# When GpSimd's adds wait for VectorE's low parts, and later work comes in halves: a two-layer graph kernel on one core

## The reference

```python
def _gcn_layer(x, adj, W, b):
    d_inv_sqrt = (jnp.sum(adj, axis=1) + 1e-09) ** (-0.5)
    msg = d_inv_sqrt[:, None] * adj * d_inv_sqrt[None, :] @ x
    return jax.nn.relu(msg @ W + b)
H_f = _gcn_layer(feature_x, adj, W_f, b_f)      # feature_x is x
H_s = _gcn_layer(spatial_x, adj, W_s, b_s)
attn = jax.nn.sigmoid(jnp.concatenate([H_f, H_s], axis=1) @ W_att + b_att)
x = _layernorm(x + attn * H_f + (1.0 - attn) * H_s)
# x, spatial_x: 4096 x 128, W_f, W_s: 128 x 128, all float32
```

## Time and profile before

| | us |
|---|---|
| median of 3 runs | 392.65 (392.62 to 392.72) |
| profiled execution | 393.04 |
| its span | 391.2 |
| PE busy in the span | 378.3 (97%) |
| DVE / ACT / POOL busy | 303.2 / 285.6 / 155.3 |

### The profile page before, as it was taken

One profiled execution on the slowest core, in us unless ns is written; L12 is line 12 of the kernel. 1 busy time (PEld: TensorE's weight loads), 2 busy tenths in 40 slices (PEclk: granted clock), 3 DMA queues, 4 the chain that ended last, 5 costly groups with the idle time before them and its releaser, 6 DMA issues. The chain is left out here.

```text
span 391.2 us, 5501 instructions
## 1 busy us (share of the span) xinstructions
PE 378.3 (97%) x1778; PEld 314.0 (80%) x1778; DVE 303.2 (77%) x443; ACT 285.6 (73%) x381; POOL 155.3 (40%) x204
## 2 busy tenths in 40 slices
PE   7889999999999999999999999999999999999992
PEld 7667778788888888788888888888788888888992
DVE  2789997999578975769578583928976796889795
ACT  3668788888877887878878887778742666687556
POOL 2332611571066402670058220010100417877795
PEclk9999999999999999999999999999999999999997
DMA  8999999999999999999999999999775534445002
GB/s 268 423 417 424 420 412 421 423 419 418 421 416 421 423 418 420 421 420 422 418 423 420 424 414 423 413 390 415 232 281 208 213 108 160 164 157 168 4 25 81
DMA packets 24556, 130.77 MB, mean 334 GB/s; under 512 B 2640, under 2 KB 7632, under 8 KB 10448
## 3 DMA queue, kind: packets, MB, share of 16 engines
q1 hardware_dynamic: 24528, 130.43, 83.2%
HBM read 128.32 MB, written 2.10 MB: 333 GB/s over the span
## 5 line engine op out<-in xcount | busy, mean ns | idle before, releaser
L533 DVE TENSOR_TENSOR Al<-raw,Ah 128x2048 fp32r<-128x2048 f32 (+2 forms) x101 | 162.0, 1620 | 40.3 <-ACT Ah L721 40.2
L408 PE MATMUL sums<-Ah,Yh 128*128 128x512 f32 (+1 forms) x484 | 186.9, 386 | 1.3 <-DVE Al L533 1.3
L409 PE MATMUL sums<-Ah,Yl 128*128 128x512 f32 (+1 forms) x484 | 185.1, 382 | 0.0
L410 PE MATMUL sums<-Al,Yh 128*128 128x512 f32 (+1 forms) x484 | 185.0, 382 | 0.0
L721 ACT ACTIVATE Ah<-raw 128x2048 fp32r<-128x2048 f32 (+2 forms) x101 | 127.1, 1283 | 48.9 <-DMA raw<-in_At 29.9
L731 ACT ACTIVATE nat<-nat 128x2048 f32<-128x2048 f32 (+1 forms) x54 | 100.1, 1855 | 20.0 <-DMA nat<-in_adj 19.3
L408 PEld LDWEIGHTS sums<-Ah,Yh 128*128 128x128 f32 x484 | 91.0, 188 | 22.5 <-DVE Al L533 4.8
L410 PEld LDWEIGHTS sums<-Al,Yh 128*128 128x128 f32 x484 | 91.0, 188 | 17.9
L409 PEld LDWEIGHTS sums<-Ah,Yl 128*128 128x128 f32 x484 | 91.0, 188 | 17.1
L553 DVE TENSOR_TENSOR acc<-sums,acc 128x512 f32<-128x512 f32 (+1 forms) x122 | 76.8, 673 | 28.8 <-PE sums L410 25.2
L871 POOL TENSOR_TENSOR S<-S,raw 128x512 f32<-128x512 f32 x40 | 62.4, 1559 | 32.2 <-DMA raw<-in_At 29.2
(11 more groups left out here) (56 smaller groups left out, 201.2 us busy)
## 6 DMA issues: line engine op xcount, KB each, us to landing
raw<-in_At SPq DMA_DIRECT2D x63, 1024.0 KB, 9.8
nat<-in_adj SPq DMA_DIRECT2D x47, 1024.0 KB, 12.0
nat<-in_adj SPq DMA_DIRECT2D x8, 768.0 KB, 9.6
xs<-in_xs SPq DMA_DIRECT2D x5, 512.0 KB, 11.1
out<-xs SPq DMA_DIRECT2D x15, 128.0 KB, 1.8
xs<-in_xs SPq DMA_DIRECT2D x5, 256.0 KB, 11.5
nat<-in_adj SPq DMA_DIRECT2D x2, 512.0 KB, 6.6
raw<-in_At SPq DMA_DIRECT2D x2, 512.0 KB, 8.5
```

The source lines that it names most:

```text
L408: pe.matmul(to, Yh[:, t % YRING, hs], high, start=first, stop=False)
L409: pe.matmul(to, Yl[:, t % YRING, hs], high, start=False, stop=False)
L410: mm = pe.matmul(to, Yh[:, t % YRING, hs], low, start=False, stop=last)
L533: dve.tensor_tensor(Al[:, k % SPLITS, a * IB:b * IB], raw[:, k % RAWS, a * IB:b * IB], Ah[:, k % SPLITS, a * IB:b * IB], ALU.subtract).the ...
```

## The change

Five things change:

1. In items under 14 that have adds, POOL waits before the first add: for Yl of the item's new tile where it has one (items 2, 6, 11, 13), otherwise for all low parts of the items before it (items 1, 5, 10, 12).
2. In items under 14 with a new tile, Ah and Al are made in four pieces of 512 instead of 512, 512, 1024.
3. Items 22 to 49 are made in two pieces of 1024 instead of one of 2048, and PE takes their first block in `first_block`. `HALVED` is split in two names for this: `BY_BLOCK` (22) for the order of sweeps and evacuations, `IN_PARTS` (50) for the pieces.
4. x of groups 3 to 7 is loaded three items later: after items 22, 29, 37, 46, 48 instead of 19, 26, 34, 43, 45.
5. Around item 48 DVE's order changes: one run (`LATE`, run 55) is evacuated last, the low parts of tiles 24 to 27 are made two in item 47 after its second half and two in item 48 after its second half, and other evacuations go behind the first half.

```diff
-HALVED = 22
+BY_BLOCK = 22
+IN_PARTS = 50
@@ sweeps
-            while k >= HALVED and n < len(items[k]) and items[k][n][0] == items[k][i][0]:
+            while k >= BY_BLOCK and n < len(items[k]) and items[k][n][0] == items[k][i][0]:
@@ order of evacuations
-    evac_order = sorted(range(len(runs)), key=lambda e: done_no[e, 0])
+    LATE = next(e for e in range(len(runs)) if end_item[e] == FINAL - 3 and runs[e][2] == 3)
+    evac_order = sorted(set(range(len(runs))) - {LATE}, key=lambda e: done_no[e, 0])
+    evac_order.insert(1 + max(evac_order.index(e) for e in evac_order if end_item[e] == FINAL - 1), LATE)
@@ loads of x
-    X_AFTER = {y_position(m * GT) - 4: m for m in range(3, G)}
+    X_AFTER = {y_position(m * GT) - 1: m for m in range(3, G)}
@@ pieces
-            if k == 0:
+            if k == 0 or k < STEPWISE and y_at[k]:
                 return [(i, i + 1) for i in range(GT)]
             if k < STEPWISE:
                 return [(0, 1), (1, 2), (2, GT)]
-            return [(0, 2), (2, GT)] if k < HALVED else [(0, GT)]
+            return [(0, 2), (2, GT)] if k < IN_PARTS else [(0, GT)]
@@ TensorE
-                    in_first = k < HALVED and j == 0
+                    in_first = k < IN_PARTS and j == 0
@@ VectorE
-                if k < HALVED:
+                if k < BY_BLOCK:
                     evacuate_new(ending[:2])
...
                     low(k, a, b)
                     if a == 0:
-                        if k >= HALVED and len(ending) == GT:
+                        if k >= BY_BLOCK and len(ending) == GT:
                             evacuate_new(ending[:2])
-                        if k in (FINAL - 1, FINAL):
-                            evacuate_new(ending[:1])
-                        for r in y_at[k]:
+                        if k == FINAL:
+                            evacuate_new(ended)
+                        if k != FINAL - 1:
+                            for r in y_at[k]:
+                                y_low(r)
+                    elif k == FINAL - 1:
+                        evacuate_new(ending[:1])
+                        for r in y_at[k][:2]:
+                            y_low(r)
+                    elif k == FINAL:
+                        for r in y_at[k - 1][2:]:
                             y_low(r)
...
-                if k < HALVED or k in (FINAL - 1, FINAL):
+                if k < BY_BLOCK:
                     evacuate_new(ending)
+                if k == FINAL:
+                    evacuate_new(ending + [LATE])
...
-                    evacuate_new(ended)
+                    evacuate_new([e for e in ended if e != LATE])
@@ GpSimd
+                if k < STEPWISE and summed_blocks(k):
+                    if y_at[k]:
+                        pool.wait_ge(Yl_ok, y_at[k][-1] + 1)
+                    else:
+                        pool.wait_ge(low_ok, GT * k)
                 for j in summed_blocks(k):
                     sum_block(k, j)
```

More of the change, by code:

```diff
@@ L658, in _ @@
                     if a == 0:
-                        if k >= HALVED and len(ending) == GT:
+                        if k >= BY_BLOCK and len(ending) == GT:
                             evacuate_new(ending[:2])
-                        if k in (FINAL - 1, FINAL):
-                            evacuate_new(ending[:1])
-                        for r in y_at[k]:
+                        if k == FINAL:
[9 more added lines that the diff above has]
+                        for r in y_at[k - 1][2:]:
                             y_low(r)
                     third_now = a == (1 if k < STEPWISE else 0) and items[k][0][0] != items[k][1][0]
-                    if k < HALVED and third_now:
+                    if k < BY_BLOCK and third_now:
                         evacuate_new(ending[:3])
-                if k < HALVED or k in (FINAL - 1, FINAL):
+                if k < BY_BLOCK:
                     evacuate_new(ending)
+                if k == FINAL:
+                    evacuate_new(ending + [LATE])
                 if k == COLLECT + 2:
```

## The result

The changed kernel takes 395.16 us in the median of seven runs (393.78 to 396.96), the kernel before 392.65 (392.52 to 392.88) beside it: ratio 1.0069, 95% interval 1.0056 to 1.0083. It is slower by 2.5 us, outside the forecast range, and its executions spread over 3.2 us where those of before lie within 0.4. The profiled one took 394.65 with a span of 392.8, 1.6 more than before.

What follows compares the result with a forecast made beforehand. TensorE (PE), at 97% of the span, was taken as the bound, with only its waits to win. Terms -0.14 - 0.21 + 0.43 + 0.96 - 0.81 - 0.27 = -0.04 took 392.65 to 392.6 us; range 390.9 to 393.7.

Steps and rivals of the forecast that it cites:

- What was called wrong ahead: Signs of error: item 14 starting under 92 or over 94.5, item 14 not waiting, or item 27 still waiting.
- Items 2 to 7: Sum of PE's waits there: -0.14 us, item 2 gaining 0.92, item 3 losing 1.56; bounds -1.0 and +0.7.
- Item 7's +0.67: Item 6's adds delay VectorE's last two Al, so PE loses 0.94 us at item 7 instead of 0.27.
- rival C: VectorE's unbroken row keeps the port and adds slip into pauses; early waits won until landings stop it: 389.8 us, chance 0.06.
- Items 10 to 14: Moved adds and the late degree delay low parts: -0.21, +0.43 and +0.96 sum to +1.18 us; bounds 0 and +1.8.
- Items 22 to 49: Two pieces of 1024 cost VectorE 0.1 us an item, hidden by idle time; later pieces together -1.08, bounds -1.15 and 0.
- -0.81 at item 27: Halves let PE start some 1.9 us earlier and x no longer lands ahead, so item 27's wait goes.
- -0.27 at item 48: The first Al has four fewer instructions ahead, ends near 276.5 against a need at 281; the 0.27 us wait goes.
- B: Late adds cost VectorE no more than early ones, so items 12 to 14 lose nothing: 391.2 us, chance 0.25.
- E: Adds have no part in the long Al and Yl, so moving them changes nothing: 391.6 us, chance 0.02.
- A: The forecast itself: 392.6 us, own range 391.9 to 393.3, chance 0.48.
- D: Slower: item 3's lag is not absorbed and passes to items 4 to 7: 393.6 us, chance 0.19.

Runs made afterwards that it cites:

- r1: The changed kernel once more, with nothing altered: 396.16 us (394.78 to 396.43).
- r9: The changed kernel with items 30 to 43 in whole pieces again: 393.56 us (393.32 to 394.94), ratio 1.003.
- r5: The kernel before plus GpSimd's waits in items 2, 5 and 6 alone: 392.58 us, ratio 1.0.
- r15: The kernel before plus later x, halves in items 22 to 29 and 44 to 49, the order at 48 and GpSimd's wait in item 20 alone: 391.59 us.
- r4: The kernel before plus only the halves in items 22 to 49, later x and the order at item 48: 393.50 us (391.60 to 395.42).
- r6: The kernel before with x of groups 3 to 7 loaded three items later, nothing else: 392.47 us, ratio 0.9999.
- r7: The kernel before plus later x, the order at 48 and halves in items 22 to 49 except item 43: 393.87 us (392.10 to 395.28).
- r10: The kernel before with items 42 and 43 alone in halves: 392.72 us (392.66 to 392.95).
- r13: The kernel before plus waits in items 2, 5, 6, 20, later x, order at 48, halves in 22 to 29, 37 to 49: 391.68 to 392.00 or 393.15 to 393.62.
- r2: The kernel before plus GpSimd's waits in items under 14 alone: 394.04 us, ratio 1.003.
- r14: The kernel before plus all waits under item 14 and in 20, later x, halves in 22 to 29 and 44 to 49, order at 48: 392.86 us.
- r12: The changed kernel with items 30 to 43 whole and GpSimd's waits in items 2, 5 and 6 alone: 392.20 us.

## Why the prediction was wrong

**Its frame held.** PE was the bound; the table accounts for the whole 1.6 of the spans by PE's waits. What was called wrong ahead did not come: item 14 starts at 93.08, waits 0.66 at its second pair, and item 27 does not wait. All these signs lay where the sum had a term; most of the loss came where it had none.

**Items 2 to 7** were taken at -0.14 and measured -1.1 at item 8 in the first profile. Items 2 (5.97, forecast 6.08) and 3 (7.34, forecast 7.29) came as worked out, and items 4 to 6 at 5.44. Item 7's +0.67 failed in this execution, where VectorE kept the port in item 6; in r1 and r9, with the same instructions up to there, it came (6.26 and 6.31), and item 8 starts at 59.76 and 59.97 where the forecast has 60.01. A second weakness is that early terms were added to the sum as if they stayed. r5 and r15 show that what the waits win before item 8 is nearly all gone by item 12. The prediction had such a limit in rival C alone.

**Items 10 to 14** were taken at +1.18, the largest single term, and its mechanism is the one seen: two adds on the low parts of each item, the degree slipping behind them, four evacuations and an Al in one row ahead of item 14. The row came on time: item 13's Al end at 90.77 (90.8 forecast), item 14 starts at 93.08 (93.14), and its Al pair at 94.36 (its first Al was to end at 94.35). Item 15 starts at 99.49, where the sum has 98.44 - 0.14 + 1.18 = 99.48. The 2.1 is larger than 1.18 because TensorE came to item 10 1.05 early and waited longer for the same low parts, in items 12 and 13 above all (0.51 and 0.53 over). So this error and that of items 2 to 7 are one and cancel. That they do so to 0.01 is luck: item 15 starts at 99.71 in r1 and 99.83 in r9, and the trace of before is 0.5 to 0.7 later there than r4, r6, r7 and r10. The degree took 1.68 for 0.80 but ended only 1.16 later, within the 1.3 that the prediction gave it.

**Items 22 to 49** are the step that failed. "Al in two of 1024 costs VectorE 0.1 an item and ScalarE as much; [...] they hide it" counted an instruction's length and not what stands around it. A split puts evacuations between the halves and lets two adds in (item 35, 0.9), and with it TensorE's order in the first block delays the evacuation that the column sums wait for (item 42, 0.5). r9 gives 1.6 of the median of 395.16 for items 30 to 43, or 2.6 by r1's 396.16. The -0.81 at item 27 and -0.27 at item 48 came, but r6 shows that later x alone does the first.

**The clock** was in no rival. After the pause of 2.2 at the collection the granted clock fell in two of six profiles, for 1.6. It carries the upper half of the changed kernel's executions (396.1 to 397.0 against 393.8 to 395.2), as far as r1's profile and r13's two groups (4 of 12 executions in the upper) allow to say; the single timed runs have no trace.

**Item 19** was counted as nothing too. With x gone from the queue the adds there start earlier and meet Yl: in r6, where x alone was moved, it takes 6.33. The waits of items 10 to 13 can do the same with x where it was, as VectorE comes there later: 6.41 in r2, 5.44 in r5. The changed kernel has both, and no run tells their shares.

**The rivals.** B, E and A are out: the adds cost what the row at 24.26 said or more. C came true in item 6, in some executions; its start of item 9 at 63.8 was nearly what r5 (63.70) and r14 (63.53) reached with most of items 2 to 7 won. D named the right sign with a wrong mechanism: item 3's lag was absorbed. Put together afterwards from the traces and experiments, the sum for the median would have been -0.2 (early), +1.5 (items 10 to 14), +0.4 (item 19), -0.9, +0.9, +0.5, -0.3 and about half of 1.6 for the clock: +2.7, against 2.5 measured (3.4 in r1). The terms are sized by the same runs, so the agreement is no test.

## What to carry to other kernels

Where two engines share a port, list for each moved instruction what it will lie beside then, and count a split as two chances to collide. What is won ahead of a stretch in which loads land at fixed times, and other work starts with them, can be gone behind it, so look for the next such stretch before adding a gain to the sum. Take a second profile of the kernel before: here one trace was 0.6 later at item 15 than four others with the same instructions up to there. And when the executions of a kernel fall into groups, look for a place where a few tenths decide, or for a pause just ahead of a fall of the clock, before reading a median.

## What the hardware showed that I had not expected

- After a pause of 2.12 to 2.19 us between block matmuls, in which only 16 small ones run, the granted clock fell to the lower level in two of six profiles (0.59 of full speed over 256 to 260 in r1); r13's upper group, 4 of 12 executions, is put down to it without a trace. With 1.70 or 1.82 it did so in no profile here, nor does any of the 96 runs of the kernel before lie in such a group.
- Early on, the clock also fell in some profiles, 0.83 over 10 to 20 in r1 and r5 against 1.00 in the changed kernel's first. Item 0 then takes 7.6 instead of 6.0, and item 3 starts at the same time all the same (30.24 and 30.08 against 30.00): VectorE paces there.
- Who gets the port is not settled by who waits. The add at 24.54 came between VectorE's instructions, the one at 47.12 in the same arrangement was kept out for three of them. In item 6 of r1 and r9 it came in, in r12 it was kept out, and in all four traces it was issued 0.15 or 0.16 after the first of the three. No run here tells why; I leave it open.
